# GpSimd halts behind runs of gathers in the first two batches of a recommender tower

## The chip, the cores and the metric

The kernel runs on one core of one Trainium2 chip. The metric is the device time of one execution in microseconds. The time of the kernel before is the median of three runs.

## The reference

A tower of a recommender model over 2048 samples. Sixteen embedding tables give one row of 256 floats for each sample; a compressed interaction network of three layers works on these 16 x 256 blocks, and a three-layer perceptron follows. In layer 0 every pair of embedding rows is multiplied element by element, and 256 products are mixed down to 16 channels; layers 1 and 2 do so with the sums of the layer before.

```python
e = jnp.stack([tbl_0[ids[:, 0]], ..., tbl_15[ids[:, 15]]], axis=1)
xk = x
for i in range(n_layers):
    z = jnp.einsum('bfe,bge->bfge', x, xk).reshape(B_, F_ * F_, E_)
    z = jnp.swapaxes(z, 1, 2)
    z = jnp.einsum('bcl,oc->bol', z, Ws[i]) + bs[i][None, :, None]
    z = jax.nn.relu(z)
    z = jnp.sum(z, axis=-1)
    outs.append(z)
    xk = jnp.broadcast_to(z[:, :, None], (B_, F_, E_))
z = jnp.concatenate(outs, axis=1)
h = jnp.concatenate([z, dense_ctx], axis=1)
h = jnp.maximum(h @ W_top1 + b_top1, 0.0)
h = jnp.maximum(h @ W_top2 + b_top2, 0.0)
y = h @ W_top3
```

## The kernel before

For each batch GpSimd (`pool`) issues 16 gathers, one for each table: an indirect DMA that brings 128 rows of 1 KB into `x_rows`. Four consecutive tables form a quarter (`QF` = 4, `NQ` = 4); the gathers of a quarter raise `gathered[par][q]` by 16 each, where `par` is the parity of the batch. For each quarter q and each half of the 256 columns TensorE transposes four 128 x 128 blocks (`transpose_tile`, L753) into one bank of `t_ps` and raises `transposed` by one. `tile(b, q, half)` is the running number of such a tile, 8 for a batch, so that "wait for `transposed`, `tile(b, q, half) + 1`" means: all tiles up to this one are there. ScalarE copies each tile to `xt` (L536) and raises `copied`. VectorE multiplies a quarter, read from `t_ps`, with an earlier quarter in `xt` (L398, 128 x 2048, raising `multiplied`): six units u0 to u5 for a batch, in two halves each. The units are the quarter pairs (1,0), (2,0), (2,1), (3,0), (3,1), (3,2). The pairs inside a quarter are made by VectorE in batch 0 (`inner_pairs_first`, L411) and by GpSimd later (`inner_pairs`, L337). Squares are ScalarE's (L544). TensorE contracts each of these parts with the weights into `z_ps` (L790) and raises `contracted`; ScalarE rectifies, TensorE sums, and so on through layers 1 and 2 and the perceptron. Product buffers form a ring of three; a new tile goes to a bank of `t_ps` only when ScalarE has copied the former one and, from the second quarter on, VectorE has multiplied with it (L745 to L751).

The start: two small loads on SyncE's queue (the ids of batch 0 and the identity), then, once the first quarter has landed, the other ids and six setup loads, and once the last quarter of batch 0 has landed six loads for the perceptron (L287 to L303). TensorE keeps itself busy with 28 and 22 dummy transposes around tiles (0,0) of batch 0, goes on with tiles (0,1,0), (0,1,1) and (0,2,0), waits for the setup loads, and enters the loop with tile (0,2,1). ScalarE copies (0,0,0), (0,0,1), (0,1,1), (0,1,0), (0,2,0), each as soon as `transposed` has its number, then waits for the setup loads. VectorE makes the inner pairs of quarter 0, then the first half of u0 straight from the bank when `transposed` has reached 3, then the second half once ScalarE has made its third copy (that of (0,1,1)).

GpSimd issues 16 gathers of batch 0, 16 of batch 1 and the first four of batch 2 in one run; its next work is `inner_pairs(1, 0, ...)`, which waits for TensorE's contraction of part i0 of batch 0. From there on gathers come four at a time with products of inner pairs between them.

Of the kernel before, what the change touches and what calls it, by code (L numbers as in the profile page):

```python
# [13 lines left out]
NF = 16  # L14
# [4 lines left out]
QF = NF // NQ  # L19
# [36 lines left out]
def build(nc, tables, ids, w0t, w12t, bias0, bias12, dense, w1, b1, w2, b2, w3,  # L56
# [10 lines left out]
    with ExitStack() as ctx:  # L67
# [6 lines left out]
        def sem(name):  # L74
            return ctx.enter_context(nc.semaphore(name))
# [43 lines left out]
        transposed = sem("transposed")  # L119
# [7 lines left out]
        contracted = sem("contracted")  # L127
# [26 lines left out]
        def tile(b, q, half):  # L154
            return TILES * b + HALVES * q + half
# [4 lines left out]
        def part(b, name):  # L160
            return NPARTS * b + (LAST_PARTS if b == LAST else PARTS).index(name)
# [19 lines left out]
        def last_unit():  # L181

            return x_rows[:, (LAST - 1) % 2, :, :].rearrange("p (h f) e -> p h (f e)", h=HALVES)
# [8 lines left out]
        def z_count(b, layer):  # L192

            n = 2 * NF * b + NF * layer
            return n - vector_count(b, layer)

        def vector_count(b, layer):

            return sum(n for (back, at), n in VECTOR_SUMS.items() if (NB - back, at) <= (b, layer))
# [85 lines left out]
        @block.sync  # L285
        def _(sp):
            sp.dma_start(ids_sb[:, 0:NF], ids[:, 0:NF]).then_inc(ids_first, 16)  # L287
            sp.dma_start(ident[:, :], identity).then_inc(ident_loaded, 16)
            sp.wait_ge(gathered[0][0], GATHER)
            sp.dma_start(ids_sb[:, NF:], ids[:, NF:]).then_inc(ids_loaded, 16)  # L290
            sp.dma_start(w0_sb[:, :, :, :], w0t).then_inc(setup_loaded, 16)
            sp.dma_start(bias0_sb[:, :], bias0).then_inc(setup_loaded, 16)
            sp.dma_start(sel0_sb[:, :, :], sel0).then_inc(setup_loaded, 16)
            sp.dma_start(w12_sb[:, :, :], w12t).then_inc(setup_loaded, 16)
            sp.dma_start(bias12_sb[:, :, :], bias12).then_inc(setup_loaded, 16)
            sp.dma_start(fold_sb[:, :], fold).then_inc(setup_loaded, 16)
            sp.wait_ge(gathered[0][NQ - 1], GATHER)
            sp.dma_start(feat[KH - ND:KH, :], dense).then_inc(mlp_loaded, 16)
            sp.dma_start(w1_sb[:, :], w1).then_inc(mlp_loaded, 16)
            sp.dma_start(b1_sb[:, :], b1).then_inc(mlp_loaded, 16)  # L300
            sp.dma_start(w2_sb[:, :, :], w2).then_inc(mlp_loaded, 16)
            sp.dma_start(b2_sb[:, :], b2).then_inc(mlp_loaded, 16)
            sp.dma_start(w3_sb[:, :], w3).then_inc(mlp_loaded, 16)  # L303
            for t in range(NT):
                sp.wait_ge(turn_moved, mlp_turn(t, MLP_STEPS - 1) + 1)
                sp.dma_start(y_out[:, t * MC:(t + 1) * MC], y_row[:, :]).then_inc(stored, 16)
            for g in range(len(TAIL_GROUPS)):
                lo, hi = tail_columns(g)
                wait_tail_moved(sp, g, MLP_STEPS - 1)
                sp.dma_start(y_out[:, NT * MC + lo:NT * MC + hi], y_row[:, lo:hi]).then_inc(stored, 16)  # L310
            sp.wait_ge(stored, 16 * (NT + len(TAIL_GROUPS)))

        @block.gpsimd
        def _(pool):
            def gather(b, first, last):

                if not b < NB:
                    return
                par = b % 2
                for f in range(first, last):  # L320
                    if b >= 2 and (f == first or f % QF == 0):
                        pool.wait_ge(transposed, tile(b - 2, f // QF, 1) + 1)
                    pool.indirect_dma_start(  # L323
                        out=x_rows[:, par, f, :], out_offset=None, in_=tables[f],
                        in_offset=bass.IndirectOffsetOnAxis(ap=ids_sb[:, NF * b + f:NF * b + f + 1].bitcast(U32), axis=0),
                    ).then_inc(gathered[par][f // QF], 16)

            def inner_pairs(b, pair, apart):

                pool.wait_ge(copied, tile(b, 2 * pair + 1, 1) + 1)  # L330
                pool.wait_ge(contracted, part(b - 1, f"i{pair}") + 1)
                x = xt[:, b % 2, :, 2 * pair * QF:(2 * pair + 2) * QF, :].rearrange("p h (q i) s -> p h q (i s)", i=QF)
                q = 1 if pair == 0 and b in VECTOR_INNER else 0
                for d in apart:
                    at = sum(QF - nearer for nearer in range(1, d)) * P
                    n = (QF - d) * P
                    pool.tensor_tensor(intra[:, pair, :, q:, at:at + n], x[:, :, q:, 0:n],  # L337
                                       x[:, :, q:, d * P:d * P + n], ALU.mult).then_inc(intra_done, 1)

            def multiply_last_unit(half):  # L340

                q, r = UNITS[NU - 1]
                pool.wait_ge(copied, tile(LAST, q, half) + 1)
                pool.wait_ge(transposed, tile(LAST - 1, NQ - 1, 1) + 1)
                pool.tensor_tensor(
                    last_unit()[:, half, :].rearrange("p (f g s) -> p f g s", f=QF, g=QF),
                    xt[:, LAST % 2, half, q * QF:(q + 1) * QF, :].unsqueeze(2).to_broadcast([P, QF, QF, P]),
                    xt[:, LAST % 2, half, r * QF:(r + 1) * QF, :].unsqueeze(1).to_broadcast([P, QF, QF, P]),
                    ALU.mult).then_inc(pool_multiplied, 1)

            def outer_last(layer):

                if layer == 1:
                    pool.wait_ge(y_copied, 1)
                    pool.wait_ge(z0_moved, NB)
                pool.wait_ge(z_ready, z_count(LAST, layer - 1))
                pool.wait_ge(vector_summed, vector_count(LAST, layer - 1))
                o = NF - LAST_OP
                y = y_last[:, :, :, layer - 1, :].rearrange("p f c o -> p o (f c)")
                pool.tensor_tensor(  # L360
                    outer[:, o // OP, o % OP:o % OP + LAST_OP, :].rearrange("p o (f g) -> p o f g", f=NF),
                    y.unsqueeze(3).to_broadcast([P, LAST_OP, NF, NF]),
                    z_all[:, LAST % 2, layer - 1, :].unsqueeze(1).unsqueeze(1).to_broadcast([P, LAST_OP, NF, NF]),
                    ALU.mult).then_inc(pool_outer, 1)

            pool.wait_ge(ids_first, 16)
            gather(0, 0, NF)
            pool.wait_ge(ids_loaded, 16)
            gather(1, 0, NF)
            gather(2, 0, QF)  # L370
            for b in range(1, NB):
                inner_pairs(b, 0, (1,))
                gather(b + 1, QF, 2 * QF)
                inner_pairs(b, 0, (2, 3))
                gather(b + 1, 2 * QF, 3 * QF)
                inner_pairs(b, 1, (1,))
                gather(b + 1, 3 * QF, NF)
                inner_pairs(b, 1, (2, 3))
                gather(b + 2, 0, QF)
            multiply_last_unit(0)  # L380
            multiply_last_unit(1)
            outer_last(1)
            outer_last(2)
# [674 lines left out]
```

## Time and profile before

| | us |
|---|---|
| median of 3 runs | 604.71 |
| lowest and highest run | 603.44, 604.8 |
| span of the profiled execution, first to last instruction | 612.3 |
| VectorE busy in it | 551.6 |
| ScalarE busy | 496.0 |
| TensorE busy | 482.5 |
| GpSimd busy | 470.3 |

The span is from the first to the last instruction of the kernel; what lies around it (starting the engines, closing down) comes on top and is not in the page. The profiled execution's own time is thus at least its span. An engine is idle either because an instruction waits for a semaphore, which the timeline shows with the engine that released it, or, where the profile has no event that explains the release, under "issue", "remote" or "another core or an unknown queue".

### The profile page before, as it was taken

Reading aid. Unit: us, or ns where it says so; the run is one execution under the profiler, and the core shown is the slowest. Engines: PE = TensorE matmul, PEld = TensorE weight load, DVE = VectorE, ACT = ScalarE, POOL = GpSimd, SP = SyncE. Lnnn points to the kernel's source line nnn. Section 1 sums busy time; section 2 is a strip of 40 time slices with the busy share of each in tenths; the row PEclk is TensorE's granted clock in tenths of the full one; section 3 lists DMA queues with packets and bytes.
Section 4 is the critical chain, followed back from the end, with each engine's and each line's share of the span. In section 5 each row is a group of like instructions: output and inputs, shape, how many; then the busy total and the mean of one; then the engine's idle time right before and its main releaser. Section 6 shows DMA issues by size and latency. Waiting matters only on the chain.

```text
span 612.3 us, 10749 instructions
## 1 busy us (share of the span) xinstructions
PE 482.5 (79%) x4014; PEld 195.0 (32%) x4014; DVE 551.6 (90%) x326; ACT 496.0 (81%) x1427; POOL 470.3 (77%) x354
## 2 busy tenths in 40 slices
PE   6124887768786888878879779898988879888988
PEld 5001232323232333323233223333333323333345
DVE  1046999999999999999999999999999999899995
ACT  1001449799989989899989899999989898999876
POOL 6771068887888888888888888888888888885911
PEclk9556999999899989999999999989999888989998
DMA  3530012221222222222222212222122221120000
GB/s 99 154 106 26 1 51 57 67 68 47 60 70 61 61 57 66 69 65 58 61 62 70 64 57 61 62 70 68 56 60 61 69 70 56 50 70 1 2 1 0
DMA packets 14332, 35.41 MB, mean 58 GB/s; under 512 B 5493, under 2 KB 5879, under 8 KB 14266
## 3 DMA queue, kind: packets, MB, share of 16 engines
q0 software_dynamic: 12288, 33.57, 19.2%
q1 hardware_dynamic: 1994, 1.17, 0.7%
q8 instruction: 32, 0.52, 0.3%
q14 instruction: 18, 0.15, 0.1%
HBM read 34.71 MB, written 0.01 MB: 57 GB/s over the span
## 4 chain that ended last, share of the span: by engine, by line
DVE 36%; POOL 22%; issue 21%; ACT 9%; PE 9%; another core or an unknown queue 2%; DMA 1%; ACTq 0%; DVEq 0%
DVE prod L398 29%; POOL x_rows L323 13%; POOL intra L337 9%; DVE outer L446 5%; ACT outer L599 4%; PE z_ps L790 4%; ACT xt L536 1%; PE t_ps L753 1%; ACT sq L544 1%; ACT outer L589 1%; PE turn_ps L854 1%; PE zs_ps L891 1%; DVE outer L464 1%; ACT relu L555 1%
## 5 line engine op out<-in xcount | busy, mean ns | idle before, releaser
L398 DVE TENSOR_TENSOR prod<-t_ps,xt 128x2048 f32<-128x2048 f32 x190 | 420.7, 2279 | 34.6 <-issue 25.5
L323 POOL DMA_INDIRECT x_rows<-in_tbl,ids_sb x256 | 246.7, 964 | 71.8 <-issue 68.2
L599 ACT ACTIVATE outer<-outer,bias_sb 128x256 f32<-128x256 f32 x487 | 241.4, 512 | 5.2 <-DVE outer L446 5.2
L337 POOL TENSOR_TENSOR intra<-xt 128x1024 f32<-128x1024 f32 (+4 forms) x90 | 210.2, 2354 | 43.1 <-PE z_ps L790 35.1
L790 PE MATMUL z_ps<-prod,w_sb 128*32 128x512 f32 x1520 | 190.3, 614 | 33.5 <-DVE prod L398 27.0
L536 ACT ACTIVATE xt<-t_ps 128x512 f32<-128x512 f32 x128 | 75.1, 602 | 69.3 <-issue 29.1
L446 DVE TENSOR_TENSOR outer<-y_ps,z_all 128x1536 f32<-128x1536 f32 (+2 forms) x66 | 110.5, 1717 | 7.4 <-ACT outer L589 4.7
L753 PE MATMUL t_ps<-ident,x_rows 128*128 128x128 f32 x512 | 82.7, 292 | 36.6 <-issue 23.2
L599 ACT ACTIVATION_READ_ACCUMULATOR outer<-outer,bias_sb 128x1 f32 x487 | 99.7, 205 | 0.0
L753 PEld LDWEIGHTS t_ps<-ident,x_rows 128*128 128x128 f32 x512 | 57.1, 145 | 99.1 <-issue 81.5
L790 PEld LDWEIGHTS z_ps<-prod,w_sb 128*32 128x32 f32 x1520 | 46.5, 111 | 122.2 <-issue 98.3
L555 ACT ACTIVATE relu<-z_ps,bias_sb 128x512 f32<-128x512 f32 (+1 forms) x80 | 52.9, 667 | 24.7 <-PE zs_ps L805 16.0
L589 ACT ACTIVATE outer<-y_ps,z_all 128x256 f32<-128x256 f32 x116 | 60.9, 694 | 0.0
L544 ACT ACTIVATE sq<-xt 128x2048 f32<-128x2048 f32 x32 | 59.5, 1918 | 0.0
L805 PE MATMUL zs_ps<-relu,sel_sb 128*32 128x128 f32 x608 | 33.6, 283 | 20.4 <-ACT relu L555 17.6
L790 PE MATMUL z_ps<-intra,w_sb 128*32 128x384 f32 x512 | 49.2, 500 | 0.4 <-ACT relu L555 0.4
L790 PE MATMUL z_ps<-sq,w_sb 128*32 128x512 f32 x256 | 37.0, 702 | 10.1 <-ACT sq L544 10.1
L823 PE MATMUL turn_ps<-xt,w_sb 128*32 128x512 f32 x256 | 30.4, 592 | 0.0
L805 PEld LDWEIGHTS zs_ps<-relu,sel_sb 128*32 128x32 f32 x608 | 14.1, 108 | 44.5 <-ACT relu L555 30.6
L854 PE MATMUL turn_ps<-feat,w_sb 64*128 64x512 f32 x24 | 15.9, 746 | 12.6 <-ACT h L620 11.3
L790 PEld LDWEIGHTS z_ps<-intra,w_sb 128*32 128x32 f32 x512 | 16.2, 111 | 25.6 <-issue 21.1
L858 PE MATMUL turn_ps<-h,w_sb 128*128 128x512 f32 x48 | 22.8, 603 | 0.0
(61 smaller groups left out, 202.7 us busy)
## 6 DMA issues: line engine op xcount, KB each, us to landing
x_rows<-in_tbl,ids_sb POOLq DMA_INDIRECT x256
w_sb<-in_w SPq DMA_DIRECT2D x1, 512.0 KB
feat<-in_dense SPq DMA_DIRECT2D x1, 128.0 KB
w_sb<-in_w SPq DMA_DIRECT2D x1, 128.0 KB
ids_sb<-in_ids SPq DMA_DIRECT2D x1, 120.0 KB
ident<-in_identity SPq DMA_DIRECT2D x1, 64.0 KB, 1.9
w_sb<-in_w0t SPq DMA_DIRECT2D x1, 64.0 KB
sel_sb<-in_sel SPq DMA_DIRECT2D x1, 48.0 KB
```

Source lines behind the costliest of these rows:

```text
L323: pool.indirect_dma_start(out=x_rows[:, par, f, :], out_offset=None, in_=tables[f], in_offset=bass.IndirectOffsetOnAxis(ap=ids_sb[:, NF * ...
L337: pool.tensor_tensor(intra[:, pair, :, q:, at:at + n], x[:, :, q:, 0:n], x[:, :, q:, d * P:d * P + n], ALU.mult).then_inc(intra_done, 1)
L398: dve.tensor_tensor(prod[:, m % PROD_RING, half, :].rearrange("p (f g s) -> p f g s", f=QF, g=QF), t_ps[:, tbank(b, q, half), :, :].unsque ...
L446: dve.tensor_tensor(outer[:, o // OP, o % OP:o % OP + n, :].rearrange("p o (f g) -> p o f g", f=NF)[:, :, :, 0:m], y.unsqueeze(3).to_broad ...
L536: act.activation(xt[:, b % 2, half, q * QF:(q + 1) * QF, :], t_ps[:, tbank(b, q, half), :, :], ACT.Copy).then_inc(copied, 1)
L544: act.activation(sq[:, half, :], xt[:, b % 2, half, :, :].rearrange("p f s -> p (f s)"), ACT.Square).then_inc(squared, 1)
L555: act.activation(relu0[:, m % 2, 0:n], z_ps[:, m % 2, 0:n], ACT.Relu, bias=bias0_sb[:, :]).then_inc(rectified, 1)
L589: act.activation(out[:, :, :, g], y, ACT.Copy, scale=z_all[:, b % 2, layer - 1, g:g + 1]).then_inc(sliced, 1)
L599: act.activation(outer[:, o // OP, o % OP, :], outer[:, o // OP, o % OP, :], ACT.Relu, bias=bias12_sb[:, layer - 1, o:o + 1], accum_out=z_ ...
L753: mm = pe.transpose(t_ps[:, tbank(b, q, half), i, :], x_rows[:, par, q * QF + i, half * P:(half + 1) * P], ident[:, :])
L790: mm = pe.matmul(z_ps[j * GR:(j + 1) * GR, m % 2, 0:n], w0_sb[:, half, slot, :], src[:, half, j * n:(j + 1) * n], start=(slot == 0 and hal ...
L805: mm = pe.matmul(zs_ps[c * GR:(c + 1) * GR, 0:P], sel0_sb[:, weights_of(pairs_of(b)[k]), :], relu0[:, m % 2, c * P:(c + 1) * P], start=(k ...
```

## The change

Only GpSimd's stream is changed, and in it only the part ahead of its loop. The 36 gathers stay the same and in the same order. Ahead of six of them stands a new wait: after 12 gathers for tile (0,1,1) of batch 0, after 16 for (0,2,1), after 20 for (0,3,0), after 24 for (0,3,1), after 28 for the contraction of part u2 of batch 0, and after 32 for tile (0,1) of batch 1. Twelve gathers of batch 0 still go out in one run; the split of them in two calls issues nothing new. The waits on `ids_first` and `ids_loaded` stay where they were.

```diff
             pool.wait_ge(ids_first, 16)
-            gather(0, 0, NF)
+            gather(0, 0, 2 * QF)
+            gather(0, 2 * QF, 3 * QF)
+            pool.wait_ge(transposed, tile(0, 1, 1) + 1)
+            gather(0, 3 * QF, NF)
+            pool.wait_ge(transposed, tile(0, 2, 1) + 1)
             pool.wait_ge(ids_loaded, 16)
-            gather(1, 0, NF)
+            gather(1, 0, QF)
+            pool.wait_ge(transposed, tile(0, 3, 0) + 1)
+            gather(1, QF, 2 * QF)
+            pool.wait_ge(transposed, tile(0, 3, 1) + 1)
+            gather(1, 2 * QF, 3 * QF)
+            pool.wait_ge(contracted, part(0, "u2") + 1)
+            gather(1, 3 * QF, NF)
+            pool.wait_ge(transposed, tile(1, 0, 1) + 1)
             gather(2, 0, QF)
             for b in range(1, NB):
                 inner_pairs(b, 0, (1,))
```

## Rows read from the trace of the kernel before

**Rows 1.** The page's first lines: span, then busy time of each engine.

```profile
span 612.3 us, 10749 instructions
PE 482.5 (79%) x4014; PEld 195.0 (32%) x4014; DVE 551.6 (90%) x326; ACT 496.0 (81%) x1427; POOL 470.3 (77%) x354
```

**Rows 2.** Busy time by stage: stretch, length, engines' busy us, clock, DMA share, GB/s.

```profile
0.00:52.00 52.00, 16.42 (x94) 11.72 (x94) 8.56 (x10) 4.16 (x6) 34.91 (x40) 0.70 0.41 113
52.00:94.00 42.00, 32.62 (x275) 12.34 (x276) 42.00 (x24) 17.65 (x27) 12.41 (x12) 0.84 0.09 24
94.00:580.00 486.00, 405.62 (x3474) 155.78 (x3475) 476.36 (x233) 452.60 (x1321) 417.61 (x301) 0.97 0.20 59
```

**Rows 3.** Chain that ended last, first 95 us: start, length, what.

```profile
11.77 29.10 issue
...
41.95 9.39 another core or an unknown queue
...
52.00 8.88 DVE prod L398 x4
```

**Rows 4.** Timeline of TensorE, 0 to 82 us: start, length, engine, line, operation [idle before].

```profile
14.68 1.09 PE L753 MATMUL t_ps<-ident,x_rows 128*128 128x128 f32 x8 [1.88 <-DMA x_rows<-in_tbl,ids_sb]
19.79 1.11 PE L753 MATMUL t_ps<-ident,x_rows 128*128 128x128 f32 x4 [4.01 <-DMA x_rows<-in_tbl,ids_sb]
42.05 1.09 PE L753 MATMUL t_ps<-ident,x_rows 128*128 128x128 f32 x4 [21.15 <-issue]
```

**Rows 5.** Timeline of VectorE, 0 to 82 us.

```profile
11.80 1.89 DVE L411 TENSOR_TENSOR intra<-xt 128x768 f32<-128x768 f32 x3 [10.66 <-issue]
31.07 2.29 DVE L398 TENSOR_TENSOR prod<-t_ps,xt 128x2048 f32<-128x2048 f32 x1 [17.37 <-issue]
41.49 2.29 DVE L398 TENSOR_TENSOR prod<-t_ps,xt 128x2048 f32<-128x2048 f32 x1 [8.14 <-issue]
43.70 1.89 DVE L411 TENSOR_TENSOR intra<-xt 128x768 f32<-128x768 f32 x3
52.00 8.88 DVE L398 TENSOR_TENSOR prod<-t_ps,xt 128x2048 f32<-128x2048 f32 x4 [6.41 <-ACT xt L536]
```

**Rows 6.** Timeline of ScalarE, 0 to 82 us.

```profile
11.17 0.60 ACT L536 ACTIVATE xt<-t_ps 128x512 f32<-128x512 f32 x1 [0.57 <-PE t_ps L753]
40.87 1.08 ACT L536 ACTIVATE xt<-t_ps 128x512 f32<-128x512 f32 x2 [29.10 <-issue]
51.37 0.60 ACT L536 ACTIVATE xt<-t_ps 128x512 f32<-128x512 f32 x1 [9.42 <-remote]
53.55 1.08 ACT L536 ACTIVATE xt<-t_ps 128x512 f32<-128x512 f32 x2 [1.59 <-remote]
```

**Rows 7.** Timeline of GpSimd, 0 to 90 us: gathers 1, 12, 13, 36, the next work.

```profile
2.62 1.12 POOL L323 DMA_INDIRECT x_rows<-in_tbl,ids_sb  x1 [2.16 <-DMA ids_sb<-in_ids]
...
16.99 0.94 POOL L323 DMA_INDIRECT x_rows<-in_tbl,ids_sb  x1 [0.30 <-issue]
18.24 0.94 POOL L323 DMA_INDIRECT x_rows<-in_tbl,ids_sb  x1 [0.30 <-issue]
...
47.04 0.95 POOL L323 DMA_INDIRECT x_rows<-in_tbl,ids_sb  x1 [0.30 <-issue]
79.41 1.83 POOL L337 TENSOR_TENSOR intra<-xt 128x768 f32<-128x768 f32 x1 [31.42 <-PE z_ps L790]
```

**Rows 8.** Timeline of all engines, 83 to 100 us.

```profile
83.94 0.41 PE L805 MATMUL zs_ps<-relu,sel_sb 128*32 128x128 f32 x6
...
85.19 0.95 POOL L323 DMA_INDIRECT x_rows<-in_tbl,ids_sb  x1 [0.30 <-issue]
...
87.16 0.28 ACT L562 ACTIVATE zs_sb<-zs_ps 128x128 f32<-128x128 f32 x1 [3.88 <-remote]
...
90.30 1.12 PE L753 MATMUL t_ps<-ident,x_rows 128*128 128x128 f32 x4
...
91.45 0.60 ACT L536 ACTIVATE xt<-t_ps 128x512 f32<-128x512 f32 x1 [0.84 <-PE t_ps L753]
```

## The prediction

> **What bounds the kernel now.** I read the page's busy times first, then the busy time by stage, then the chain that ended last, and last the timelines of the start, engine by engine. VectorE is busy for 551.6 of 612.3 us [rows 1], and from 94 to 580 us it is busy for 476.36 of 486 [rows 2]: the middle of the kernel is VectorE's and has next to nothing to give. From 52 to 94 us it is busy without a gap (42.00 of 42). What is left is the start: in the first 52 us VectorE works for 8.56 us. The chain says the same, and says it oddly: 29.10 us of "issue" from 11.77, and 9.39 us of "an unknown queue" from 41.95, then VectorE's products [rows 3].
>
> The timelines tell what these gaps are. TensorE transposed tiles (0,1,0) and (0,1,1) at 14.68, all eight pieces done at 15.77, and (0,2,0) at 19.79, done at 20.90 [rows 4]. VectorE's first product needs `transposed` to be 3, so it could start at 15.3 or so, but starts at 31.07. ScalarE's third copy needs 4, ready at 15.77, and starts at 40.87; its fifth needs 5, ready at 20.90, and starts at 51.37 [rows 5, 6]. So three signals of TensorE, in order, arrive some 16, 25 and 30 us late, 9.8 and 10.5 us apart. No data is missing. Signals of VectorE and ScalarE come at once: VectorE's second half starts 0.02 us after the first of ScalarE's two copies (40.87 + 0.60 = 41.47), and TensorE's tile (0,2,1) 0.10 us after the second (40.87 + 1.08 = 41.95). Through all of it GpSimd issues gathers without a pause, from 2.62 to 47.99 us, one each 1.25 us [rows 7]; the backlog is gone 3.4 to 5.6 us after its last (51.37 and 53.55). Later on, gathers come four at a time, and there the signals are far less late: a transposition that ends at 91.42 amid gathers is copied at 91.45, while a sum that ends at 84.35 is taken up at 87.16, 2.8 us late and 1.0 after the fourth gather, which ended at 86.14 [rows 8]. That a long run of gathers holds back TensorE's signals is thus what the profile suggests; it has no row that names the cause.
>
> **The change, step by step.** It adds six waits to GpSimd and no work. Behind each of them stand only gathers, then the inner pairs of batch 1. Those who wait for the gathers are TensorE's transposes, and SyncE's perceptron loads, which wait for the last quarter of batch 0 and are used many batches later.
>
> The first halt comes after gather 12, at 16.99 + 0.94 = 17.93 us [rows 7]. Signals 3 and 4 then come between at once (17.9) and with the lag that the end of the long run shows: 17.93 + 3.38 = 21.3 for one, + 5.56 = 23.5 for the next [rows 6, 7]. From signal 4 to the first product of u1 the engines need 0.62 + 2.21 + 1.89 = 4.7 us (40.87 to 45.59: copy, second half of u0, inner pairs) [rows 5, 6]. If both signals come at once, one product of 2.29 stands ahead of it: 17.9 + 2.29 + 2.29 + 1.89 = 24.4. With the whole lag: 23.5 + 4.7 = 28.2. Before it was 52.00 [rows 5], so the start shrinks by 23.8 to 27.6 us.
>
> Signal 5 (tile (0,2,0)) may stay behind until the second halt: four more gathers are 5.0 us, and 3.4 of lag: 23.5 + 5.0 + 3.4 = 31.9, u1 at 32.5, and 19.5 us gained. The row at 91.45 says that within four gathers a signal may be prompt, that at 87.16 that it may lose 2.8 us [rows 8]. For the four later halts I take nothing at the low end, and 2.8 us for each of four runs, 11, at the high end, if each fell on VectorE's path. Gain in the profile: 8 to 28 us, taken as 22, since most of the stall is in the three signals, and VectorE has work queued in between. GpSimd itself: 24 gathers after the first halt take 30 us, so it ends at some 54 us plus halts, while the inner pairs of batch 1 would come due at 79.41 - 22 = 57.4. That it is idle 31.42 us there [rows 7] is what covers the halts now; with the stall gone the cover is about 3 us, and past that GpSimd would be late.
>
> So the span of the changed kernel in a profile would be 612.3 - 22 = 590.3 us.
>
> **From the profile to the timed runs.** The profiled execution is slower than the timed ones: its own time is 612.3 plus what lies around, the median is 604.71. So being profiled costs 7.6 us plus what lies around, and outside the stall there is little that could bear it: VectorE has only 9.6 us of idle time between 94 and 580 us [rows 2]. The stall is therefore shorter in a timed run. If nothing lay around the span, the stall would be 7.6 shorter and the gain 22 - 7.6 = 14.4 us: 590.3. If 14.4 us or more lay around it, nothing would be left to gain: 604.7. I know neither end from a row and take the middle, 7.2 us: 597.5.
>
> The Trainium skill has a figure for what lies around: the page "Runtime: NRT & Kernel Launch" (section on the preamble/postamble breakdown) gives 9 to 15 us. No row here shows it. By it, an estimate, the sum would be 590.3 + 9 to 15 = 599 to 605, nearer to no change.
>
> **The rivals.**
>
> *Nothing changes.* The late signals belong to the profiled execution: where every instruction leaves a record, a queue of records can hold up TensorE's signals while gathers run. For it: the profiled execution is the slower one by more than 7.6 us; between signals 4 and 5 only four transposes and their four weight loads lie, and they took 10.5 us, about one of these eight for each gather. Against it: ScalarE's and VectorE's signals are prompt beside the same gathers. Then the halts never bind, each signal being there before the gathers ahead of it are out: 604.7.
>
> *The whole stall is in the timed runs too.* What the profile costs then lies elsewhere, in the 9.6 us of idle time in the middle [rows 2] for one. The gain is the whole 22 us: 582.7.
>
> *Slower.* Mechanism: the timed run has little stall, so batch 0 already comes as early as 52.0 - 24.4 = 27.6 us ahead of the profile; the inner pairs of batch 1 are due at 79.41 - 27.6 = 51.8, and GpSimd's run of 36 gathers ends at 47.99 [rows 7]. The cover is 3.8 us. Six halts that each last the 3.4 us of lag would be 20 us, so GpSimd comes to its first inner pairs up to 16 us late. It decides once the halts together pass 3.8 us. GpSimd is busy for 417.61 of 486 us in the middle [rows 2], so it wins back only 14% of a stretch, and TensorE's contraction of inner parts, then the rings behind it, would wait. A quarter of the 16 us reaching VectorE gives 4 us: 608.7. Against it: the halts wait for tiles that TensorE makes early.
>
> **How the numbers follow.** The forecast, a part of the stall won back (gain over 2 us, up to 14), 0.52: 597.5. The whole gain, 0.14: 582.7. Nothing changes, 0.21: 604.7. Slower, 0.13: 608.7. The predicted time is that of the likeliest, 597.5. For eight in ten I take all of the forecast (590 to 602.9), no change (to 606), and half of the case of the whole gain, from 584: the range is 584 to 606. About 0.3%, 1.8 us, is what a measurement can tell. Faster by more: 0.52 + 0.14 = 0.66. Within: 0.21. Slower: 0.13.
>
> **What the profile after would show.** Right: GpSimd has gaps after 12, 16, 20, ... gathers; ScalarE's third copy starts between 18 and 24 us in place of 40.87; VectorE is busy without a gap from about 25 to 32 us on, in place of 52; span near 590; GpSimd reaches its first inner pairs near 57, with its idle time ahead of them nearly gone. Wrong: the third copy still comes at 40 or the halts themselves last 10 us and more, since then a pause of GpSimd isn't what lets signals through; or VectorE gets new gaps between 30 and 90 us behind tiles of batch 1. And if the span shrinks by 20 us while the timed runs stay at 604, the stall was the profile's own.

## The result, and the profile after

The changed kernel takes 589.31 us (median of four runs, 585.88 to 591.23) where the kernel before takes 604.75 on the same chip (603.44 to 609.29). The ratio is 0.972, 95% interval 0.967 to 0.978: 15.4 us, 2.6%, faster. The forecast was 597.5; the direction and the place were right and the gain was 15.4 us where I had put down 7.2.

The experiments then showed something that matters more than the number: in this comparison and in two of six later jobs the kernel before takes 604 to 607 us; in the four other jobs, on other chips, it takes 574, and in the one of them in which the changed kernel ran it gives nothing.

The page of the changed kernel (busy time of each engine) and its stages (length, then busy time of TensorE, its weight loads, VectorE, ScalarE, GpSimd; granted clock; DMA share; GB/s):

```profile
span 583.8 us, 10751 instructions
PE 483.6 (83%) x4014; PEld 195.3 (33%) x4014; DVE 550.9 (94%) x326; ACT 496.6 (85%) x1427; POOL 469.4 (80%) x354
...
0.00:52.00 52.00, 33.29 (x204) 17.16 (x205) 34.12 (x25) 11.79 (x15) 33.84 (x39) 0.80 0.39 106
52.00:94.00 42.00, 32.55 (x324) 13.80 (x326) 39.43 (x22) 31.14 (x81) 33.21 (x27) 0.97 0.22 62
```

The busy time of every engine is that of before [rows 1] within 1.1 us; the span is 28.5 us shorter. In the first 52 us VectorE now works for 34.12 us, where it worked for 8.56 [rows 2].

The start of the changed kernel, timelines of GpSimd (gathers 12, 13, 25 and 33, then the first inner pairs), ScalarE and VectorE, to be held against [rows 5 to 7]:

```profile
16.89 0.95 POOL L323 DMA_INDIRECT x_rows<-in_tbl,ids_sb  x1 [0.31 <-issue]
20.01 0.94 POOL L323 DMA_INDIRECT x_rows<-in_tbl,ids_sb  x1 [2.17 <-remote]
...
36.97 0.94 POOL L323 DMA_INDIRECT x_rows<-in_tbl,ids_sb  x1 [2.25 <-remote]
...
48.54 0.95 POOL L323 DMA_INDIRECT x_rows<-in_tbl,ids_sb  x1 [1.86 <-remote]
...
56.64 1.83 POOL L337 TENSOR_TENSOR intra<-xt 128x768 f32<-128x768 f32 x1 [2.58 <-PE z_ps L801]
```

```profile
19.78 0.60 ACT L547 ACTIVATE xt<-t_ps 128x512 f32<-128x512 f32 x1 [8.10 <-remote]
...
29.52 0.60 ACT L547 ACTIVATE xt<-t_ps 128x512 f32<-128x512 f32 x1 [4.93 <-PE t_ps L764]
36.73 0.60 ACT L547 ACTIVATE xt<-t_ps 128x512 f32<-128x512 f32 x1 [6.61 <-remote]
```

```profile
19.72 4.49 DVE L409 TENSOR_TENSOR prod<-t_ps,xt 128x2048 f32<-128x2048 f32 x2 [6.11 <-remote]
24.12 1.95 DVE L422 TENSOR_TENSOR intra<-xt 128x768 f32<-128x768 f32 x3
26.00 8.87 DVE L409 TENSOR_TENSOR prod<-t_ps,xt 128x2048 f32<-128x2048 f32 x4
```

Three of the six halts bind, at gathers 13, 25 and 33, for 1.9 to 2.3 us each. Behind the first, VectorE and ScalarE get their signals together, 1.9 us after GpSimd's last gather ended (17.84), and the first product of u1 starts at 26.00 in place of 52.00. The two halts after gathers 16 and 20 find their tiles signalled already, so that gathers 13 to 24 go out in one run, and tile (0,3,1) at its end is copied only at 36.73. TensorE's timeline tells when that run begins to hold signals back:

```profile
22.80 1.08 PE L764 MATMUL t_ps<-ident,x_rows 128*128 128x128 f32 x4 [2.04 <-ACT xt L547]
24.26 2.96 PE L801 MATMUL z_ps<-prod,w_sb 128*32 128x512 f32 x16 [0.37 <-DVE prod L409]
28.32 0.66 PE L764 MATMUL t_ps<-ident,x_rows 128*128 128x128 f32 x4 [1.09 <-DMA x_rows<-in_tbl,ids_sb]
...
33.70 0.66 PE L764 MATMUL t_ps<-ident,x_rows 128*128 128x128 f32 x4
```

Tile (0,3,0), the third line, is done at 28.98 and copied at 29.52, half a microsecond later, though 24 matmuls and their weight loads have completed since 22.80 beside five gathers. Tile (0,3,1), the last line, is done at 34.36 and copied 2.4 us later. So signals pass during the first seven gathers behind a halt, and they are not let out at a fixed rate of one completing instruction for each gather, as I had read from four transposes and four loads in 10.5 us.

### The profile page after: what moved, and what is told of

It is laid out like the page before. It is cut to its first block, busy times and chain, and to the rows that moved or that the text cites. A ratio compares the mean times of both kernels' runs of the same rounds, so it can differ in the third digit from the quotient of the medians.

```text
span 583.8 us, 10751 instructions
## 1 busy us (share of the span) xinstructions
PE 483.6 (83%) x4014; PEld 195.3 (33%) x4014; DVE 550.9 (94%) x326; ACT 496.6 (85%) x1427; POOL 469.4 (80%) x354
## 4 chain that ended last, share of the span: by engine, by line
DVE 36%; ACT 27%; PE 18%; issue 12%; POOL 3%; another core or an unknown queue 2%; DMA 1%; ACTq 0%; DVEq 0%; POOLq 0%
DVE prod L409 29%; ACT outer L610 14%; PE z_ps L801 10%; DVE outer L457 6%; ACT outer L600 3%; ACT sq L555 3%; ACT relu L566 3%; POOL x_rows L323 3%; PE t_ps L764 2%; ACT xt L547 2%; PE zs_ps L816 1%; PE turn_ps L873 1%; PE turn_ps L834 1%; DMA x_rows<-in_tbl,ids_sb 1%
## 5 line engine op out<-in xcount | busy, mean ns | idle before, releaser
L610 ACT ACTIVATION_READ_ACCUMULATOR outer<-outer,bias_sb 128x1 f32 x487 | 101.1, 208 | 0.0
L816 PE MATMUL zs_ps<-relu,sel_sb 128*32 128x128 f32 x608 | 32.5, 282 | 17.0 <-ACT relu L566 14.8
L801 PE MATMUL z_ps<-sq,w_sb 128*32 128x512 f32 x256 | 38.2, 724 | 9.4 <-ACT sq L555 9.4
L865 PE MATMUL turn_ps<-feat,w_sb 64*128 64x512 f32 x24 | 14.4, 682 | 8.0 <-ACT h L631 7.7
```

The lines of the kernel that those rows point to most:

```text
L610: act.activation(outer[:, o // OP, o % OP, :], outer[:, o // OP, o % OP, :], ACT.Relu, bias=bias12_sb[:, layer - 1, o:o + 1], accum_out=z_ ...
L801: mm = pe.matmul(z_ps[j * GR:(j + 1) * GR, m % 2, 0:n], w0_sb[:, half, slot, :], src[:, half, j * n:(j + 1) * n], start=(slot == 0 and hal ...
L816: mm = pe.matmul(zs_ps[c * GR:(c + 1) * GR, 0:P], sel0_sb[:, weights_of(pairs_of(b)[k]), :], relu0[:, m % 2, c * P:(c + 1) * P], start=(k ...
```

## Experiments

The six jobs below ran on six different chips; whether the chip of the comparison above is one of them is not known. In each job the kernel before ran beside the new ones, and its time falls into one of two groups with nothing between: 604.75, 606.92 and 603.96 us, or 573.88, 574.14, 574.03 and 574.01 us. I call the chips of the first group late and those of the second prompt, for what their traces show; no chip ran twice, so that chip and job cannot be told apart. Numbers that follow are compared within one job, except where a late chip is set beside a prompt one.

### First job, a prompt chip: one halt, free pauses, more and fewer dummies

Only the first halt:

```diff
-            gather(0, 0, NF)
+            gather(0, 0, 3 * QF)
+            pool.wait_ge(transposed, tile(0, 1, 1) + 1)
+            gather(0, 3 * QF, NF)
```

> Only the first of the six halts (after gather 12, for tile (0,1,1)); the other 24 gathers go out in one run. Theory A (a pause of GpSimd lets TensorE's held signals through, and each long run holds them anew): ScalarE's third copy near 20 us as in the changed kernel, but the signals of tiles (0,2,0), (0,2,1), (0,3,0), (0,3,1) are 10 us apart again during the next 24 gathers (20 to 50 us); so only a part of the 15 us comes back, 5 to 9 us (596 to 600). Theory B (only the burst at 12 to 18 us, where setup loads and dummy transposes meet the gathers, makes the backlog): one halt is enough, 589 us as in the changed kernel.

Measured: 574.17 us against 573.88, ratio 1.000 (0.999 to 1.001). Neither theory had foreseen that the kernel before has nothing to win here. Timelines of ScalarE and of GpSimd (gathers 12 and 13) in this run:

```profile
16.68 0.60 ACT L538 ACTIVATE xt<-t_ps 128x512 f32<-128x512 f32 x1 [5.56 <-PE t_ps L755]
18.21 0.60 ACT L538 ACTIVATE xt<-t_ps 128x512 f32<-128x512 f32 x1 [0.94 <-DVE prod L400]
```

```profile
16.99 0.95 POOL L323 DMA_INDIRECT x_rows<-in_tbl,ids_sb  x1 [0.30 <-issue]
18.25 0.95 POOL L323 DMA_INDIRECT x_rows<-in_tbl,ids_sb  x1 [0.30 <-issue]
```

The halt lasts no time, since the third copy comes at 16.68 us, as soon as the tile is transposed, in the middle of an unbroken run of gathers. Gathers at the same pace hold nothing back on this chip.

Pauses tied to nobody (a scratch tile `idle_sb` and a semaphore `idled` are new; eight memsets, each behind the one before):

```diff
+            def pause():
+                for _ in range(8):
+                    pool.memset(idle_sb[:, :], 0.0).then_inc(idled, 1)
+                    idles.append(0)
+                    pool.wait_ge(idled, len(idles))
...
+            gather(0, 0, 3 * QF)
+            pause()
+            gather(0, 3 * QF, NF)
+            pause()
             pool.wait_ge(ids_loaded, 16)
+            for q in range(NQ):
+                gather(1, q * QF, (q + 1) * QF)
+                pause()
             gather(2, 0, QF)
```

> At the places of the six halts (the last after gather 32) GpSimd does eight small memsets of a scratch tile of its own, each waiting for the one before, and waits for no other engine. Theory A (what counts is that no gather is issued for a while): third copy near 20 us and 587 to 593 us, like the changed kernel. Theory C (the halts help by tying the gathers to TensorE's progress, not by the pause): no gain over the kernel before, 600 us or more.

Measured: 585.1 us, ratio 1.019 (1.017 to 1.021), 11.2 us slower. Both expectations were made for a late chip and missed. GpSimd's timeline, the first of the six pauses and the first inner pairs:

```profile
17.95 2.06 POOL L373 MEMSET idle_sb<- 128x128 f32 x8
...
61.15 1.85 POOL L339 TENSOR_TENSOR intra<-xt 128x768 f32<-128x768 f32 x1
```

In the one-halt kernel the same line stands at 49.44 us, after an idle time of only 0.58 us:

```profile
49.44 1.83 POOL L337 TENSOR_TENSOR intra<-xt 128x768 f32<-128x768 f32 x1 [0.58 <-PE z_ps L792]
```

GpSimd comes 11.7 us late and the kernel ends 11.2 us late. This is the mechanism of the prediction's slower rival, at nearly full price: where signals are prompt GpSimd waits for only 0.58 us at its first inner pairs, and that is all its cover.

The dummies, `WARM["second"]` = 44 and 0 in place of 22:

> The kernel before with 44 dummy transposes in place of 22 between the tiles (0,0) and (0,1) (computes the same). Theory D (each TensorE instruction that completes takes a slot behind the gathers, so that the signals queue behind dummies): signals 3 and 4 come later than at 31 and 41 us, by some 10 us or more, and the time rises by 5 us or more. Theory E (only signals queue, one for some eight gathers): third copy at 38 to 42 us as before, and the time is 604, within 3 us.

> The kernel before with no dummy transposes between the tiles (0,0) and (0,1) (computes the same). Theory D (dummies fill the queue ahead of the signals): signal 4 comes 10 us or more earlier than at 41 us and the kernel gains 5 to 10 us (595 to 600). Theory E (only signals queue): third copy still at 38 to 42 us and 604 us, within 3 us; a lower clock of TensorE at the start costs under 1 us.

Measured: 574.26 us (ratio 1.000, 0.999 to 1.001) and 574.95 us (1.0015, 1.0002 to 1.0029), third copy at 16.18 and 16.93 us. On a prompt chip they tell nothing of the theories D and E. Leaving the dummies out costs TensorE clock: the granted clock is 0.50 of the full 2.4 GHz, so 1.2 GHz, from 14.90 to 16.90 us without dummies, and 1.00 from 15.10 to 16.15 with 44, and the tiles (0,1,0) and (0,1,1) take 1.97 us and 1.04 (timelines of TensorE, none and 44). That the 1.1 us of the kernel's time go there is not shown; VectorE's first product comes 0.34 us later (16.08 against 15.74).

```profile
14.93 1.97 PE L753 MATMUL t_ps<-ident,x_rows 128*128 128x128 f32 x8 [4.35 <-DMA x_rows<-in_tbl,ids_sb]
```

```profile
15.11 1.04 PE L753 MATMUL t_ps<-ident,x_rows 128*128 128x128 f32 x8
```

### Second job, a late chip: the change itself, half the pause, two halts

> The changed kernel itself, beside the kernel before on the chip of this job. If TensorE's signals are prompt there, as in the job before (the kernel before at 573.88 us, ScalarE's third copy at 16.2 to 16.9 us in all its variants): each tile is signalled before the gathers ahead of its halt are out (16.7, 21.9, 26.3, 29.5, about 32 and 36.9 us against 17.9, 22.9, 27.9, 32.9, 37.9 and 42.9), so no halt binds and the ratio is 1.00 within 0.002. If the signals are late there, with the kernel before near 604 us: 586 to 591, ratio 0.97, as in the first comparison. The rival of the prediction that halts make GpSimd late: ratio 1.005 to 1.02 where the signals are prompt.

Measured: 588.19 us against 606.92, ratio 0.970 (0.965 to 0.975), inside the 586 to 591 that were expected. The first comparison holds again.

Four memsets in place of eight:

> As e2_pause_unlinked, with four memsets instead of eight at each of the six places: a pause of some 1.2 us in place of 2.3. With prompt signals, if GpSimd has no slack at its first inner pairs (it came to them at 61.15 us in place of 49.44 with the long pauses, and the time rose by 11.2): half the pause, half the loss, 5 to 6.5 us. If the loss came from another effect of the pauses, such as later gathers for one tile, it goes to under 2 us. With late signals: between the kernel before and the changed one.

Measured: 585.75 us, ratio 0.966 (0.960 to 0.972), so 2.4 us below the changed kernel in the same job. The expectation (between the kernel before and the changed one) missed low. Timelines of GpSimd (first pause), ScalarE (third copy) and VectorE:

```profile
17.87 1.01 POOL L373 MEMSET idle_sb<- 128x128 f32 x4
```

```profile
22.58 0.60 ACT L551 ACTIVATE xt<-t_ps 128x512 f32<-128x512 f32 x1 [10.86 <-remote]
```

```profile
21.14 4.49 DVE L413 TENSOR_TENSOR prod<-t_ps,xt 128x2048 f32<-128x2048 f32 x2 [7.50 <-PE t_ps L768]
...
52.95 13.27 DVE L413 TENSOR_TENSOR prod<-t_ps,xt 128x2048 f32<-128x2048 f32 x6
```

Behind pauses that are tied to nothing the signals pass too, so it is the pause that helps and not the tie. They do not pass within it: GpSimd stands for 1.27 us (17.88 to 19.15), and VectorE's first product starts at 21.14, 3.3 us after the end of gather 12 and amid the next four. ScalarE's third copy is 2.7 us later than with the halts in the same job (19.89) and the first product of u1 1.3 us later (27.36 against 26.04). But the pauses come behind every run of four, also where the halts did not bind, and VectorE runs from 21.14 us on without a gap where the changed kernel has one of 2.9 to 4.0 us near 55; that more than pays for it.

The first two halts only:

> Only the first two halts. With prompt signals: no difference, within 0.2%. With late signals (the kernel before near 604 us): they cover the signals of tiles (0,1,1), (0,2,0) and (0,2,1), the whole of the stall in the trace of before, and the 20 gathers behind them go out in one run. If the first stall is what costs, 586 to 592 us as with six; if every long run costs as much, 594 to 602.

Measured: 598.02 us, ratio 0.989 (0.982 to 0.996). This is the answer "every long run costs". VectorE's timeline:

```profile
26.04 8.87 DVE L401 TENSOR_TENSOR prod<-t_ps,xt 128x2048 f32<-128x2048 f32 x4
34.84 1.88 DVE L414 TENSOR_TENSOR intra<-xt 128x768 f32<-128x768 f32 x3
43.50 6.69 DVE L401 TENSOR_TENSOR prod<-t_ps,xt 128x2048 f32<-128x2048 f32 x3 [4.58 <-issue]
53.54 4.49 DVE L401 TENSOR_TENSOR prod<-t_ps,xt 128x2048 f32<-128x2048 f32 x2 [3.35 <-remote]
57.94 1.89 DVE L414 TENSOR_TENSOR intra<-xt 128x768 f32<-128x768 f32 x3
65.75 2.29 DVE L401 TENSOR_TENSOR prod<-t_ps,xt 128x2048 f32<-128x2048 f32 x1 [5.93 <-ACT xt L539]
```

Up to 36 us it is the changed kernel; then, behind the gathers that go out without a halt, the signals are late anew and VectorE waits three times, for 13.9 us. The four later halts are worth 9.8 us (598.02 less 588.19).

### Third and fourth job, prompt chips

The dummies again, the changed kernel, and a small gap behind every gather of batches 0 and 1:

```diff
+            def gathers(b, first, last):
+                for f in range(first, last):
+                    gather(b, f, f + 1)
+                    pool.memset(idle_sb[:, :], 0.0).then_inc(idled, 1)
+                    idles.append(0)
+                    pool.wait_ge(idled, len(idles))
...
-            gather(0, 0, NF)
+            gathers(0, 0, NF)
             pool.wait_ge(ids_loaded, 16)
-            gather(1, 0, NF)
+            gathers(1, 0, NF)
```

> The kernel of e3_more_dummies again (44 dummy transposes in place of 22), which ran on a chip where the kernel before has no late signals. Where they are late (before near 604 us): theory D (every completing TensorE instruction takes a slot behind the gathers, about one for a gather; 4 transposes and 4 weight loads took 10 us) puts ScalarE's third copy at 50 us or later, after the last gather, and the time 5 to 12 us over before; theory E (only signals take slots) leaves the copy within 3 us of 41 us and the time within 3 us of before. Where signals are prompt: the same as before, again.

> The kernel of e4_no_dummies again (no dummies between the tiles). Where signals are late: theory D puts the third copy before 35 us and the time 5 to 12 us under before; theory E leaves it within 3 us of 41 us and the time within 3 us of before. Where signals are prompt: within 0.3% of before, again.

> The changed kernel again, for the chip of this job. Where signals are prompt: no halt binds, ratio 1.000 within 0.003 (each tile is signalled before the gathers ahead of its halt are out). Where they are late: 587 to 590 us, ratio 0.97.

> No halts; one memset of a scratch tile (0.25 us) behind each of the 32 gathers of batches 0 and 1, so that the same kind of pause as in c2_half_pause is spread evenly. Where signals are late: if what counts is the share of time without a gather, they come as with c2_half_pause, 584 to 590 us; if a gap must be long enough (1 us was), the stall stays, third copy after 35 us and 600 us or more. Where signals are prompt: GpSimd comes some 8 us later to its first inner pairs and the time rises by 6 to 9 us.

Measured against 574.14 us: 44 dummies 574.1 (1.000, 0.999 to 1.001), none 575.14 (1.0015, 1.0004 to 1.0027), the changed kernel 574.66 (1.0007, 0.9996 to 1.0018), the gaps 577.78 (1.006, 1.004 to 1.008). So where signals are prompt the change is worth nothing and costs nothing: no halt binds, and GpSimd's first inner pairs stand at 49.21 us:

```profile
49.21 1.82 POOL L337 TENSOR_TENSOR intra<-xt 128x768 f32<-128x768 f32 x1 [0.58 <-PE z_ps L801]
```

The gaps make GpSimd come at 54.68 us; it costs 3.6 us, not the 6 to 9 that I had expected, also because the 32 memsets delay GpSimd by 5.3 us and not 8.

The fourth job, on another prompt chip, had the dummies and the gaps again, and a shorter pause:

> 44 dummy transposes in place of 22, a third time, for a chip where signals are late: theory D (every completing TensorE instruction takes a slot behind the gathers) puts ScalarE's third copy at 50 us or later and the time 5 to 12 us over before; theory E (only signals take slots) leaves the copy within 3 us of 41 us and the time within 3 us of before. Where signals are prompt: the same as before.

> No dummies between the tiles, for a chip where signals are late: theory D puts the third copy before 35 us and the time 5 to 12 us under before; theory E leaves it within 3 us of 41 us and the time within 3 us of before. Where signals are prompt: within 0.3% of before.

> One memset behind each of 32 gathers, for a chip where signals are late: if the share of time without a gather counts, 584 to 592 us; if a gap must be as long as 1 us, the third copy comes after 35 us and the time is 600 us or more. Where signals are prompt: 2 to 5 us over before (3.6 in the run before this one).

> Two memsets (some 0.5 us) at each of the six places of the halts, half of c2_half_pause. Where signals are late: if TensorE's held signals pass within half a microsecond, 583 to 588 us, better than the changed kernel; if a pause has to last about as long as the lag seen behind the halts (2 us behind the last gather), 595 us or more. Where signals are prompt: 0 to 3 us over before.

Measured against 574.03 us: 574.61 (1.001, 1.000 to 1.002), 575.21 (1.002, 1.001 to 1.003), 577.41 (1.007, 1.004 to 1.010) and, with six pauses of half a microsecond, 575.95 (1.003, 1.001 to 1.005).

### Fifth job, a late chip: the dummies at last

> 44 dummy transposes in place of 22, once more. Where signals are late (before near 604 us): theory D puts ScalarE's third copy at 50 us or later and the time 5 to 12 us over before; theory E leaves the copy within 3 us of 41 us and the time within 3 us of before. Where they are prompt: the same as before.

Measured: 616.85 us (616.65 and 617.05) against 603.96 (601.6 to 608.58), ratio 1.020 (1.006 to 1.034): 12.9 us slower, by 22 dummy transposes of 0.11 us each whose results nobody reads. With two runs against three the interval is wide, 3.5 to 20.7 us. The third copy comes at 53.45 us. This is theory D's side, though the loss lies just above its 5 to 12 us. Timelines of TensorE, ScalarE and GpSimd's last gather:

```profile
15.37 0.60 PE L913 MATMUL zs_ps<-ident 128*128 128x128 f32 x4 [0.54 <-issue]
16.09 0.27 PE L753 MATMUL t_ps<-ident,x_rows 128*128 128x128 f32 x1
16.81 0.54 PE L753 MATMUL t_ps<-ident,x_rows 128*128 128x128 f32 x3 [0.45 <-issue]
17.52 0.27 PE L753 MATMUL t_ps<-ident,x_rows 128*128 128x128 f32 x1 [0.17 <-issue]
18.23 0.33 PE L753 MATMUL t_ps<-ident,x_rows 128*128 128x128 f32 x1 [0.44 <-issue]
18.95 0.27 PE L753 MATMUL t_ps<-ident,x_rows 128*128 128x128 f32 x1 [0.39 <-issue]
```

```profile
53.45 0.60 ACT L536 ACTIVATE xt<-t_ps 128x512 f32<-128x512 f32 x1 [42.31 <-remote]
```

```profile
46.99 0.95 POOL L323 DMA_INDIRECT x_rows<-in_tbl,ids_sb  x1 [0.30 <-issue]
```

Two things are to be seen. The signals of the tiles, which TensorE has made by 23 us, wait until 5.5 us after the last gather. And TensorE itself is slowed: four of its dummies, which wait for nothing, stand behind an idle 0.54 us, and the transposes of tiles (0,1,0) and (0,1,1) come mostly one by one some 0.7 us apart with "issue" between them. With 22 dummies, in the trace of before, these eight came in one piece [rows 4]. On a prompt chip (job four) the kernel with 44 makes them in one piece too:

```profile
15.20 1.09 PE L753 MATMUL t_ps<-ident,x_rows 128*128 128x128 f32 x8
```

So what is held back is fed by TensorE's completing instructions, dummies too, and not by its signals alone. This rests on one trace and two runs, and the place of the copy before, 40.87, on one trace of another job, itself at 612.3 us of span against 614.5 here. That the dummies' own time, which moves the tiles 1.4 us further into the run of gathers (16.09 against 14.68), does the harm is not ruled out: the run without dummies that would tell never met a late chip.

### Sixth job, a prompt chip

> The other side of g1_more_dummies (which cost 12.9 us where signals are late, with the third copy at 53.45 us): no dummy transposes between the tiles. Where signals are late: theory D puts the third copy before 35 us and the time 5 to 12 us under before; if it is only that the dummies' own time pushes the tiles into the run of gathers, copy and time stay within 3 us of before. Where signals are prompt: within 0.3% of before.

> Two memsets (some 0.5 us) at each of the six places. Where signals are late: if the held signals pass within half a microsecond, 583 to 588 us; if a pause must last about 1 us or more, 592 or more. Where signals are prompt: 1 to 3 us over before (1.9 in the run before).

Measured against 574.01 us: 574.4 (1.000, 0.999 to 1.002) and 575.66 (1.0025, 1.001 to 1.004), GpSimd's first inner pairs at 51.88 us. Neither question was answered, since the chip was prompt.

### What the runs tell together

Place of GpSimd's first inner pairs and time, on prompt chips, against 49.4 us: short pauses +2.5 us, time +1.7; gaps +5.2, +3.6; long pauses +11.7, +11.2. A microsecond of GpSimd there costs two thirds of a microsecond of the kernel to nearly a whole one.

The traces carry a mark of the two groups beside the time. The number of semaphore updates recorded is 3628 for the kernel before, 3815 for the changed one, 3813, 3805, 3774 and 3752 in the four runs on late chips; in the fourteen traces of prompt chips it is 6351 to 6399, for the same instructions but for the edits. What is missing are mostly the updates by landing DMAs (1713 to 1895 against 4254 to 4300) and fewer of the engines' (1915 to 1944 against 2082 to 2134). In the stall nearly all are missing, whoever made them: from 12 to 48 us the trace of before has 3 updates by engines, that with 44 dummies on a late chip none, and that of one halt on a prompt chip 59. VectorE's product at 31.07 and ScalarE's copies at 40.87 are among those without a record, although VectorE's second product at 41.49 and TensorE's tile (0,2,1) at 42.05, which wait for those copies, show that the signals came through. A missing update is thus no mark of a late one, and it is why the waits stand under "issue" and "remote".

The halts do not make a late chip prompt: the changed kernel takes 588 to 589 us there and 574.66 on a prompt one. Stages of the changed kernel on the prompt chip of job three, then one of its stages in the first comparison:

```profile
0.00:52.00 52.00, 37.96 (x298) 20.62 (x298) 38.58 (x28) 15.83 (x22) 38.12 (x42) 0.90 0.41 114
52.00:94.00 42.00, 32.12 (x287) 12.87 (x284) 42.00 (x23) 32.31 (x94) 35.83 (x29) 0.92 0.22 64
94.00:540.00 446.00, 377.47 (x3262) 146.32 (x3258) 444.07 (x216) 428.34 (x1238) 389.17 (x282) 0.98 0.21 60
```

```profile
94.00:540.00 446.00, 379.30 (x3222) 145.78 (x3218) 441.15 (x213) 421.56 (x1226) 384.87 (x284) 0.96 0.21 61
```

On the late chip VectorE does 4.5 us less in the first 52 us, 2.6 less in the next 42 and 2.9 less up to 540: together 10.0 of the 10.8 us between the two spans (583.8 and 573.0). More than half of what is left lies behind the start.

Not settled: what makes a chip late; whether fewer completing instructions ahead of the tiles shorten the stall; how short a pause still helps on a late chip. And each run here, timed ones too, comes with a span and a granted clock from a record of it, so none tells whether the recording, in which the updates are missing, is part of the stall: signals held up by a crowded recorder remain the rival that no run here tests.

## Why the prediction was right and wrong

**The bound and the place** were right: the start, three held signals, VectorE idle for want of them, and the middle untouched.

**A pause lets the signals through**: right, and shown by c2_half_pause, whose pauses wait for no one. The lag behind the end of a run is 2 us at the halts and 3.3 at the short pause, in place of the 3.4 to 5.6 taken from the long run, and the fifth signal does not need a halt of its own (ScalarE's next two copies come together at 22.11). The first product of u1 came at 26.00, inside the 24.4 to 28.2 of the first sum, not at the 32.5 of the low end.

**The sum in the profile** was 22 us and the span fell by 28.5. 26.0 of these are the first product of u1, inside the 23.8 to 27.6 that I had for the start; by taking 22 I had set 1.8 to 5.6 of it aside for the fifth signal and the later halts. From that product to the end the changed kernel takes 583.8 - 26.00 = 557.8 us and the kernel before 612.3 - 52.00 = 560.3, so in these two traces the later halts cost no net time, a new gap of 2.9 us near 54 included. Between 94 and 580 us [rows 2] VectorE idled for 9.6 us; in the changed kernel's 94 to 550 it idles for 456.00 - 450.53 = 5.5:

```profile
94.00:550.00 456.00, 389.30 (x3290) 149.14 (x3282) 450.53 (x218) 430.88 (x1253) 394.87 (x288) 0.97 0.21 60
```

**From the profile to the timed runs** is the step that failed, and in it the term for what lies around the span. I took it that being profiled costs 7.6 us plus what lies around, that this cost lies in the stall, and put what lies around at 7.2 us, the middle between nothing and 14.4. It is 2.1 us: the changed kernel's run with the span of 583.8 has the time 585.88, and its others 585.5 and 587.62, 588.9 and 591.0, 589.1 and 591.23. With 2.1 in that step, the forecast would have been 590.3 + 2.1 = 592.4, which is 5.1 of the 8.2 us by which 597.5 was too slow. The other 3.1 us lie in the sum of the profile, where I took 22 us: span 590.3 forecast, 587.2 the median of the four.

That the stall was longer in the profiled execution than in the timed ones is borne out: at 612.3 + 2.1 = 614.4 us it lies above all eighteen timed runs of the kernel before in the late group (601.6 to 609.98). Whether this is a price of profiling or the far end of a spread that is 8 us wide by itself, no run tells; the changed kernel's profile is one of its timed runs, the fastest. So the 28.5 us between the two profiles are 15.4 that the timed runs show, 9.7 by which the one profile lies above its median, and 3.4 by which the other lies below.

The page "Runtime: NRT & Kernel Launch" of the Trainium skill (section on the preamble/postamble breakdown) gives 9 to 15 us around a kernel; here time less span is 2.1 us, and the measurement decides. Which of the page's stages the device time takes in, no run shows.

**The rivals.** "Nothing changes" fell on the late chips and is what happens on the prompt ones, by the mechanism named: each signal is there before the gathers ahead of it are out. Of its reason, the part that completing instructions queue behind the gathers is supported by g1_more_dummies, at no fixed rate of one for each gather; whether it is their records that queue stays open. "The whole stall is in the timed runs too", 582.7, lies 6.6 us from the result and so nearer than the forecast, but its gain of 22 us was not there either: the timed runs gained 15.4. "Slower" named the right resource, GpSimd's arrival at its first inner pairs, and e2_pause_unlinked paid its price; but the change's halts never last long enough for it: on prompt chips they take no time, on late ones GpSimd still waits 2.58 us for TensorE there. I had put the decision at 3.8 us of cover; on prompt chips it is 0.6.

## What to carry to other kernels

A wait whose releaser was done long ago, in a trace where nothing else accounts for it, can be a signal that is held up. Here the remedy was a breath in the stream that crowds it, tied to the signal itself so that it costs nothing where signals are prompt: the halts won 15 to 19 us on late chips and lost nothing clear of noise on the prompt one, while of the pauses of fixed length one kind won 2 us more on a late chip, and three others lost 2, 3.5 and 11 us on prompt ones. Dummy instructions that only keep an engine awake may not be free in such a stretch; 22 more of them went with 12.9 us (3.5 to 20.7) on the one late chip that ran them. Before the difference of one profiled execution from a median is explained, look at the spread of the runs and at time less span of any run, and repeat on a second chip what rests on one.

## What was unexpected of the hardware

The same kernel takes 574 us on four chips and 604 to 607 on two others and in the first comparison, 5% more, and most of what the traces show of it lies in how TensorE's completions travel while GpSimd issues gathers without a break. On the late chips they pass for the first gathers behind a pause (tile (0,3,0), half a microsecond late), are held in a long run for 16 to 30 us (trace of before), come 2 to 5.5 us after a run ends, and in the one trace with 44 dummies TensorE's own issue is slowed to one transpose in 0.7 us. VectorE's and ScalarE's signals are prompt in every row read here.
